# Stage one of a six-stage decoder kernel: decay weights beside the convolution, part of the sum on VectorE, out projection inside the mixing loop

## The chip, the cores and the metric

One core of one Trainium2 chip runs the whole kernel. The metric is the device time of one execution in microseconds (us). PE is TensorE, PEld its weight load, DVE VectorE, ACT ScalarE, POOL GpSimd, SP the queue that issues most transfers.

## The reference, cut to what matters

The layer is `x = layernorm(x + f(x))` six times over, with six different `f`, on x of 8 x 128 x 512 in float32. Stage one is the first: a down projection to 128 features with gelu, two applications of the same state-space layer `_hydra`, a gated mix and an up projection. The sequence axis of `_hydra` is the batch axis of x (8 steps), and the 128 positions are its batch.

```python
zxbcdt = u @ in_w.T                       # z 256, xBC 288, dt 8
dt = softplus(dt2 + dt_bias)              # forward and backward
xBC = silu(causal_conv(xBC, 7 taps))      # xs 256, B 16, C 16
y_fw, y_bw = scans(xs, dt, A, B, C)       # over 8 steps, shifted by one
y = y_fw + y_bw + xs * repeat(xs @ fcD_w.T + D, 64)
yz = y * silu(z)
y = yz * rsqrt(mean(yz**2) + 1e-5) * norm_w
return y @ out_w.T                        # next layer's u
```

With 8 steps the scans are written out: y of step t is the sum over the 8 steps s of xs[s] times one weight per (t, s, head), built from B, C and exponentials of summed dt.

## The kernel before

The six stages follow one another with a barrier of all engines between them. Only `hydra_stage` (stage one) is touched. In it the 128 partitions are the positions and a "token" t is one of the 8 steps. In each of two layers (a hardware loop on every engine), in this order on TensorE:

- z and dt of token t (L268) and the convolution of token t (L275, up to seven matmuls accumulated, weights that GpSimd multiplied together at L239), t from 0 to 7, two PSUM banks each. ScalarE takes z through silu (L336) and dt out (L337), VectorE adds the bias (L382), ScalarE takes silu of the result (L339).
- Transposes of xs (L284), copied out by ScalarE (L344), and the skip products (L289).
- Meanwhile VectorE makes the weights: softplus (L386 to L400), distances (L403 to L407), exponents (L408, L411), exp on ScalarE (L347), B times C (L414, L416), decays times dt (L419), fourteen small products along diagonals (L431, L432), skip (L435).
- The mixing loop: for token t VectorE multiplies all of xs by the weights (L442, 128 x 2048, two buffers), TensorE adds the eight products by eight matmuls with the identity (L298), VectorE multiplies by z (L448), ScalarE squares and sums (L352).
- After all eight tokens: mean square (L450), power -0.5 on GpSimd (L248), scaling (L453), transposes of y (L306), copies with norm_w (L356), out projection of both halves (L311), copies to uT (L360). Then layer 1 begins.

After layer 1 VectorE forms x times 2 plus the up bias (L456), mixes (L461, L462), TensorE projects up (L319), VectorE adds (L466). Meanwhile, in layer 0, GpSimd splits the context for stage two into a high and a low part (L243, L245), four pieces of 1024 columns each.

A matmul in full float32 is two instructions in the records, so eight matmuls are "x16". All waits are semaphores on constants or loop registers; the order on each engine is the order written.

Of the kernel before, what the change touches and what calls it, by code (L numbers as in the profile page):

```python
# [11 lines left out]
ACT = mybir.ActivationFunctionType  # L12
AX = mybir.AxisListType.X

P = 128
B, S, D = 8, 128, 512
# [121 lines left out]
def hydra_stage(nc, m, io, sem):  # L138
    with ExitStack() as ctx:
# [3 lines left out]
        def pb(name, n=HALF):  # L143
            return ctx.enter_context(nc.psum_tensor("hy_" + name, [P, n], FP32))

        xT0 = m.pre[:, :].rearrange("p (c n) -> p c n", c=KC)
# [18 lines left out]
        uT = sb("uT", [P, TOK])  # L165
        z_act = sb("z_act", [P, L, DIN])
# [11 lines left out]
        prod = [sb(f"prod{i}", [P, L, DIN]) for i in range(2)]  # L178
        yz = sb("yz", [P, L, DIN])
# [4 lines left out]
        yT = sb("yT", [P, 2, TOK])  # L184
# [4 lines left out]
        ld = {n: sem("hy_ld_" + n) for n in ("x", "gelu", "in", "conv", "small", "up", "ctx", "kv")}  # L189
        s = {n: sem("hy_" + n) for n in (  # L190
            "ident", "consts", "mid", "mid_act", "u", "wconv", "alpha", "alpha_exp", "a_exp", "na", "z_mm",
            "z_out", "c_mm", "c_out", "xbc", "xs_tr", "xs_T", "skip", "chain", "pool", "sp_in", "sp_exp",
            "seg", "dec", "w_ok", "prod", "y_mm", "yz", "ssq", "msq", "rms", "yn", "y_tr", "y_T", "o_mm",
            "mixed", "up_mm", "xres", "resid", "c_hi", "c_lo")}

        with nc.Block() as block:
            @block.sync
            def _(sp_):
                for c in range(KC):
                    sp_.dma_start(xT0[:, c, :], io["xT"].rearrange("(c p) n -> p c n", p=P)[:, c, :]).then_inc(ld["x"], 16)  # L200
                sp_.dma_start(w_down[:, :, :], io["w_downT"].rearrange("(c p) n -> p c n", p=P)).then_inc(ld["gelu"], 16)
                sp_.dma_start(b_down[:, :], io["b_down"].rearrange("(p a) -> p a", a=1)).then_inc(ld["gelu"], 16)
                sp_.dma_start(w_zdt[:, 0:DIN], io["in_wT"][:, 0:DIN]).then_inc(ld["in"], 16)
# [15 lines left out]
            def _(pool):  # L219
                pool.dma_start(taps[:, :, :], io["conv_w"].partition_broadcast(P)).then_inc(ld["conv"], 16)  # L220
# [19 lines left out]
                pool.wait_ge(s["consts"], 2)  # L240
                pool.wait_ge(ld["ctx"], 16)
                for c in range(KC):
                    pool.tensor_tensor(m.cT_hi[:, c:c + 1, :], xT0[:, c:c + 1, :], bc(m.ones[:, 0:1], 2, [P, 1, TOK]), ALU.mult).then_inc(s["c_hi"], 1)  # L243
                    pool.wait_ge(s["c_hi"], c + 1)
                    pool.tensor_tensor(m.cT_lo[:, c, :], xT0[:, c, :], raw(m.cT_hi[:, c, :]), ALU.subtract).then_inc(s["c_lo"], 1)  # L245
                with pool.Fori(0, LAYERS) as i:
                    pool.wait_ge(s["msq"], i + 1)
                    pool.tensor_tensor(rms[:, :], msq[:, :], m.minus_half[:, 0:L], ALU.pow).then_inc(s["rms"], 1)  # L248

            @block.tensor  # L250
            def _(pe):
                pe.wait_ge(ld["x"], 16 * KC)
                pe.wait_ge(ld["gelu"], 32)
                for h in range(2):
                    for c in range(KC):
                        last = pe.matmul(bank[h][:, :], w_down[:, c, :], xT0[:, c, h * HALF:(h + 1) * HALF],
                                         start=c == 0, stop=c == KC - 1)
                    last.then_inc(s["mid"], 1)
                pe.wait_ge(s["wconv"], 1)
                pe.wait_ge(s["ident"], 2)  # L260
                pe.wait_ge(ld["small"], 16 * 9)
                with pe.Fori(0, LAYERS) as i:
                    pe.wait_ge(s["u"], 2 * i + 2)
                    for t in range(L):

                        if t >= 2:
                            pe.wait_ge(s["z_out"], L * i + t - 1)
                        pe.matmul(bank[t % 2][:, 0:ZDT], uT[:, t * P:(t + 1) * P], w_zdt[:, :],  # L268
                                  start=True, stop=True).then_inc(s["z_mm"], 1)
                        if t >= 2:  # L270
                            pe.wait_ge(s["c_out"], L * i + t - 1)
                        first = max(0, TAPS - 1 - t)
                        for k in range(first, TAPS):
                            src = t - (TAPS - 1) + k
                            last = pe.matmul(bank[2 + t % 2][:, 0:CONV], uT[:, src * P:(src + 1) * P], w_conv[:, k, :],  # L275
                                             start=k == first, stop=k == TAPS - 1)
                        last.then_inc(s["c_mm"], 1)
                    for t in range(L):

                        pe.wait_ge(s["xbc"], L * i + t + 1)  # L280
                        if t >= 2:
                            pe.wait_ge(s["xs_T"], L * i + t - 1)
                        for c in range(2):
                            last = pe.transpose(bank[4 + t % 2][:, c * P:(c + 1) * P], xbc[:, t, c * P:(c + 1) * P], m.ident[:, :])  # L284
                        last.then_inc(s["xs_tr"], 1)
                    for t in range(L):
                        pe.wait_ge(s["xs_T"], L * i + t + 1)
                        for c in range(2):
                            last = pe.matmul(skip_bank[:, t * NH:(t + 1) * NH], xsT[:, c, t * P:(t + 1) * P], fcd[:, c, :],  # L289
                                             start=c == 0, stop=c == 1)  # L290
                    last.then_inc(s["skip"], 1)
                    for t in range(L):

                        pe.wait_ge(s["prod"], L * i + t + 1)
                        if t >= 2:
                            pe.wait_ge(s["yz"], L * i + t - 1)
                        for src in range(L):
                            last = pe.matmul(bank[t % 2][:, 0:DIN], m.ident[:, :], prod[t % 2][:, src, :],  # L298
                                             start=src == 0, stop=src == L - 1)
                        last.then_inc(s["y_mm"], 1)  # L300
                    for t in range(L):
                        pe.wait_ge(s["yn"], L * i + t + 1)
                        if t >= 2:
                            pe.wait_ge(s["y_T"], 2 * (L * i + t - 1))
                        for c in range(2):
                            last = pe.transpose(bank[2 + t % 2][:, c * P:(c + 1) * P], yz[:, t, c * P:(c + 1) * P], m.ident[:, :])  # L306
                        last.then_inc(s["y_tr"], 1)
                    for h in range(2):
                        pe.wait_ge(s["y_T"], 2 * (L * i + L))
                        for c in range(2):  # L310
                            last = pe.matmul(bank[4 + h][:, :], w_out[:, c, :], yT[:, c, h * HALF:(h + 1) * HALF],  # L311
                                             start=c == 0, stop=c == 1)
                        last.then_inc(s["o_mm"], 1)
                pe.wait_ge(ld["up"], 48)
                for b in range(B):
                    pe.wait_ge(s["mixed"], b // 4 + 1)
                    if b >= 2:
                        pe.wait_ge(s["resid"], b - 1)
                    pe.matmul(bank[b % 2][:, :], hm[:, b * P:(b + 1) * P], w_up[:, :], start=True, stop=True).then_inc(s["up_mm"], 1)  # L319

            @block.scalar
            def _(act):
                for h in range(2):
                    act.wait_ge(s["mid"], h + 1)
                    act.activation(x_mid[:, h * HALF:(h + 1) * HALF], bank[h][:, :], ACT.Gelu, bias=b_down[:, :]).then_inc(s["mid_act"], 1)
                for h in range(2):
                    act.wait_ge(s["mid_act"], h + 1)
                    act.activation(uT[:, h * HALF:(h + 1) * HALF], x_mid[:, h * HALF:(h + 1) * HALF], ACT.Copy).then_inc(s["u"], 1)
# [4 lines left out]
                with act.Fori(0, LAYERS) as i:  # L333
                    for t in range(L):
# [3 lines left out]
                        act.wait_ge(s["c_out"], L * i + t + 1)  # L338
                        act.activation(xbc[:, t, :], xbc[:, t, :], ACT.Silu).then_inc(s["xbc"], 1)  # L339
                    act.wait_ge(s["sp_in"], i + 1)  # L340
                    act.activation(sp[1][:, :], sp[0][:, :], ACT.Exp).then_inc(s["sp_exp"], 1)
                    for t in range(L):
                        act.wait_ge(s["xs_tr"], L * i + t + 1)
                        act.activation(xsT[:, :, t * P:(t + 1) * P], bank[4 + t % 2][:, 0:DIN].rearrange("p (c n) -> p c n", c=2),  # L344
                                       ACT.Copy).then_inc(s["xs_T"], 1)
                    act.wait_ge(s["seg"], i + 1)
                    act.activation(dec[:, :, :, :, :], dec[:, :, :, :, :], ACT.Exp).then_inc(s["dec"], 1)  # L347
                    for t in range(L):
                        act.wait_ge(s["yz"], L * i + t + 1)
                        if t:  # L350
                            act.wait_ge(s["ssq"], L * i + t)
# [1799 lines left out]
```

## Time and profile before

| | us |
|---|---|
| median of 3 runs (1761.96 to 1769.78) | 1765.85 |
| profiled execution, its own time | 1768.64 |
| its span | 1766.8 |
| stage one in it | 0 to 205.4 |
| PE busy over the span | 1557.7 (88%) |
| DVE, ACT, POOL busy | 923.5, 788.7, 734.9 |

Busy time is a sum over an engine; what ends a stage is read from the timeline of that stage. The granted clock (PEclk) is a share of full speed: 1.00 is 2.4 GHz, 0.50 is 1.2 GHz.

### The profile page before, as it was taken

The numbers are of one execution on the slowest core, as the hardware profiler recorded it, in microseconds if no ns is written. First come the engines' busy times: TensorE is split into PE (matmuls) and PEld (weight loads), VectorE is DVE, ScalarE is ACT, GpSimd is POOL, SyncE is SP. The second block draws the span as 40 slices with busy tenths as digits, with TensorE's granted clock in tenths as the row PEclk, the third lists the DMA queues.
The fourth block names the chain that finished last, engine by engine and source line by source line (L and its number), as shares of the span: only waits on it lengthen the run. The fifth ranks groups of instructions, "written<-read, shape, count | busy, mean of one in ns | idle before, by whom it ended". The sixth has DMA issues, their size and how long they took to land. (4 is left out here: it accounts for less than half of the span.)

```text
span 1766.8 us, 28778 instructions
## 1 busy us (share of the span) xinstructions
PE 1557.7 (88%) x10647; PEld 1286.8 (73%) x10647; DVE 923.5 (52%) x1621; ACT 788.7 (45%) x2417; POOL 734.9 (42%) x589
## 2 busy tenths in 40 slices
PE   5888799999997699986999648999999999999836
PEld 3767497888885478875777437888888888888724
DVE  0627611333346588773567724555555555556644
ACT  2231223444443355534899714545545445445400
POOL 4100113444422599843533544555554555542210
PEclk9888899999999799998999859999999999999978
DMA  6100100100100643104000040101100110000011
GB/s 197 36 0 0 36 19 19 38 19 21 45 6 1 213 163 125 36 1 150 1 2 25 25 132 25 37 25 37 48 28 34 37 37 25 25 1 1 1 42 48
DMA packets 63474, 77.74 MB, mean 44 GB/s; under 512 B 13884, under 2 KB 43052, under 8 KB 63340
## 3 DMA queue, kind: packets, MB, share of 16 engines
q1 hardware_dynamic: 60860, 74.36, 13.3%
q8 instruction: 84, 1.38, 0.3%
q0 software_dynamic: 464, 1.32, 0.3%
q10 hardware_dynamic: 2016, 0.27, 0.1%
q14 instruction: 50, 0.41, 0.1%
HBM read 73.85 MB, written 2.10 MB: 43 GB/s over the span
## 5 line engine op out<-in xcount | busy, mean ns | idle before, releaser
L989 POOL TENSOR_TENSOR xa_rs<-xa_ms,minus_half 128x5 f32<-128x5 f32 x64 | 74.7, 1167 | 171.4 <-DVE xa_ms L1211 171.4
L972 POOL TENSOR_TENSOR xa_prob<-xa_prob,xa_inv 128x512 f32<-128x512 f32 x64 | 66.6, 1040 | 138.3 <-DVE xa_inv L1178 138.3
L605 POOL TENSOR_TENSOR xa_prob<-xa_prob,xa_inv 128x1024 f32<-128x1024 f32 x32 | 60.6, 1895 | 142.2 <-DVE xa_inv L859 142.2
L1156 ACT ACTIVATE xa_prob<-xa_prob,xa_peak 128x128 f32<-128x128 f32 x256 | 99.8, 391 | 42.5 <-DVE xa_peak L1222 42.5
L1206 DVE TENSOR_REDUCE xa_ssq<-xa_qn 128x4 f32<-128x512 f32 x64 | 43.9, 686 | 136.4 <-ACT xa_qn L1142 136.4
L1502 DVE SCALAR_TENSOR_TENSOR ff_acc<-ff_ring,ff_sT,ff_acc 128x512 f32<-128x512 f32 x140 | 100.4, 747 | 21.9 <-ACT ff_acc L1456 12.7
L71 PE MATMUL xa_qp<-xa_q_hi,xT_hi 128*128 128x512 f32 x256 | 108.0, 422 | 1.7 <-DVE xa_q_lo L1169 1.7
L1406 PE MATMUL ff_ring<-xT_hi,ff_w 128*128 128x512 f32 x224 | 93.0, 415 | 17.9 <-DVE ff_acc L1502 11.6
L71 PE MATMUL xa_rows<-xa_o_hi,xa_out_hi 128*128 128x512 f32 x256 | 101.6, 397 | 5.2 <-DVE xtok L1185 5.2
L1884 ACT ACTIVATE sa_work<-sa_work,sa_peak 128x128 f32<-128x128 f32 x256 | 99.1, 393 | 10.3 <-DVE sa_peak L1921 10.2
L72 PE MATMUL xa_qp<-xa_q_hi,xT_lo 128*128 128x512 f32 x256 | 102.4, 400 | 0.0
L73 PE MATMUL xa_rows<-xa_o_lo,xa_out_hi 128*128 128x512 f32 x256 | 102.2, 399 | 0.0
L73 PE MATMUL xa_qp<-xa_q_lo,xT_hi 128*128 128x512 f32 x256 | 102.0, 398 | 0.0
L1142 ACT ACTIVATE xa_qn<-xa_qp 128x512 f32<-128x512 f32 x64 | 38.2, 597 | 142.8 <-PE xa_qp L73 142.8
L72 PE MATMUL xa_rows<-xa_o_hi,xa_out_lo 128*128 128x512 f32 x256 | 101.6, 397 | 0.0
L1718 POOL TENSOR_TENSOR sa_work<-sa_work,sa_inv 128x1024 f32<-128x1024 f32 x32 | 60.7, 1898 | 93.9 <-DVE sa_inv L1925 93.7
L841 DVE TENSOR_REDUCE xa_peak<-xa_score 128x4 f32<-128x1024 f32 x32 | 39.1, 1223 | 115.6 <-PE xa_score L683 115.6
L1407 PE MATMUL ff_ring<-xT_lo,ff_w 128*128 128x512 f32 x224 | 91.7, 409 | 0.0
L71 PE MATMUL xa_kvp<-xa_kv_hi,cT_hi 128*128 128x256 f32 x256 | 78.8, 308 | 8.6 <-DVE xa_kv_lo L1164 8.6
L1456 ACT ACTIVATE ff_acc<-ff_ring,ff_sT 128x512 f32<-128x512 f32 x84 | 56.9, 685 | 49.8 <-PE ff_ring L1407 49.2
L73 PE MATMUL xa_kvp<-xa_kv_lo,cT_hi 128*128 128x256 f32 x256 | 73.3, 286 | 0.0
L72 PE MATMUL xa_kvp<-xa_kv_hi,cT_lo 128*128 128x256 f32 x256 | 73.1, 285 | 0.0
(390 smaller groups left out, 4820.9 us busy)
## 6 DMA issues: line engine op xcount, KB each, us to landing
xa_raw_q<-in_wq SPq DMA_DIRECT2D x8, 1024.0 KB, 5.4
xa_raw_o<-in_wo SPq DMA_DIRECT2D x8, 1024.0 KB, 5.3
ff_dn_q<-in_down_w SPq DMA_DIRECT2D x7, 512.0 KB, 3.5
ff_dn_z<-in_down_z SPq DMA_DIRECT2D x7, 512.0 KB, 5.1
ff_dn_s<-in_down_s SPq DMA_DIRECT2D x7, 512.0 KB, 6.5
pre<-in_wq SPq DMA_DIRECT2D x16, 192.0 KB, 3.3
pre<-in_wo SPq DMA_DIRECT2D x16, 192.0 KB, 3.7
sa_work<-in_w_qkvT SPq DMA_DIRECT2D x3, 1024.0 KB, 8.3
```

The source lines that it names most:

```text
L71: pe.matmul(out, a_hi, b_hi, start=first, stop=False)
L72: pe.matmul(out, a_lo, b_hi, start=False, stop=False)
L73: return pe.matmul(out, a_hi, b_lo, start=False, stop=last)
L605: pool.tensor_tensor(prob[:, t % 3, :, :], prob[:, t % 3, :, :], bc(inv[:, t % 3, :], 2, [P, Q, KEYS]), ALU.mult).then_inc(s["norm"], 1)
L972: pool.tensor_tensor(prob[:, u % 2, :, :], prob[:, u % 2, :, :], bc(inv[:, u % 2, :], 2, [P, Q, S]), ALU.mult).then_inc(s["norm"], 1)
L989: pool.tensor_tensor(rs[:, :], ms[:, :], m.minus_half[:, 0:Q + 1], ALU.pow).then_inc(s["rs"], 1)
L1156: last = act.activation(prob[:, u % 2, h, :], prob[:, u % 2, h, :], ACT.Exp, bias=peak[:, u % 2, h:h + 1], accum_out=total[:, u % 2, h:h + 1])
L1406: pe.matmul(bank[:, :], w[:, T % 3, c, a, f], m.xT_hi[:, c, cols], start=True, stop=False)
L1407: pe.matmul(bank[:, :], w[:, T % 3, c, a, f], m.xT_lo[:, c, cols], start=False, stop=True).then_inc(s["grp"], 1)
L1502: dve.scalar_tensor_tensor(acc[:, n % SETS, slot, :], ring[(8 * n + i) % RING][:, :], column(n, i), acc[:, n % SETS, slot, :], ALU.mult, A ...
L1718: pool.tensor_tensor(prob[:, u % 3, :, :], prob[:, u % 3, :, :], bc(inv[:, u % 3, :], 2, [P, HC, S]), ALU.mult).then_inc(s["norm"], 1)
L1884: last = act.activation(prob[:, t % 3, h, :], prob[:, t % 3, h, :], ACT.Exp, bias=peak[:, t % 3, h:h + 1], accum_out=total[:, t % 3, h:h + 1])
```

## The change

- The loads: w_down and its bias first, then x in two halves of columns instead of four chunks of rows. Each half of the down projection waits for its own half.
- Layer 0 reads the gelu output directly; the copies to uT (L328) are gone. The loops over the layers are unrolled.
- z and dt of all tokens come ahead of the convolution, which now uses four banks, with the transposes of xs three tokens behind it and the skip products five behind.
- VectorE makes softplus, distances, exponents and decays between the bias adds. ScalarE changes its function table more often for that.
- norm_w is multiplied into w_out once; x times 2 plus bias and the scaling of x_mid are done before layer 0 and layer 1.
- The context's high part is copied by ScalarE in layer 0's convolution instead of by GpSimd; GpSimd keeps the low part.
- Mixing: three product buffers; VectorE adds products 2 and 3 onto 0 and 1 (`halves`), TensorE adds the remaining six. Mean square, root, transposes, out projection and the transpose back to uT are done per token inside the loop. The root scales the projected rows (128 wide) and no longer yz.

The core of the diff (the helpers are the old operations, per token):

```diff
+                for h in range(2):
+                    cols = slice(h * HALF, (h + 1) * HALF)
+                    sp_.dma_start(xT0[:, :, cols], ...[:, :, cols]).then_inc(ld[f"x{h}"], 16)
...
+                for i in range(LAYERS):          # tensor
+                    for t in range(L):
+                        z_and_dt(i, t)
+                    if i == 0:
+                        pe.wait_ge(s["wconv"], 1)
+                        pe.wait_ge(s["w_out"], 2)
                     for t in range(L):
+                        conv(i, t)
+                        if t >= 3:
+                            turn_xs(i, t - 3)
+                        if t >= 5:
+                            skip(i, t - 5)
+                    for t in range(L - 3, L):
+                        turn_xs(i, t)
+                    for t in range(L - 5, L):
+                        skip(i, t)
+                    for t in range(L + 4):
+                        if t < L:
+                            mixed_sum(i, t)
+                        if 1 <= t < L + 1:
+                            turn_y(i, t - 1)
+                        if 3 <= t < L + 3:
+                            project_out(i, t - 3)
+                        if t >= 4:
+                            turn_u(i, t - 4)
...
+                    for t in range(L):           # scalar, after z, dt and exp of softplus
+                        silu_xbc(i, t)
+                        if i == 0 and 1 <= t <= KC:
+                            act.wait_ge(ld["ctx"], 16)
+                            act.activation(m.cT_hi[:, t - 1, :], xT0[:, t - 1, :], ACT.Copy).then_inc(s["c_hi"], 1)
+                        if t == 5:
+                            act.wait_ge(s["seg"], i + 1)
+                            act.activation(dec[...], dec[...], ACT.Exp).then_inc(s["dec"], 1)
+                        if t >= 3:
+                            out_xsT(i, t - 3)
+                    for t in range(L - 3, L):
+                        out_xsT(i, t)
+                    for t in range(1, L + 4):
+                        if t < L + 1:
+                            square(i, t - 1)
+                            out_yT(i, t - 1)
+                        if 3 <= t < L + 3:
+                            out_rows(i, t - 3)
+                        if t >= 4:
+                            out_uT(i, t - 4)
...
+                    softplus_in(i)               # vector
+                    conv_bias(i, 0)
+                    conv_bias(i, 1)
+                    softplus_out(i)
+                    conv_bias(i, 2)
+                    conv_bias(i, 3)
+                    conv_bias(i, 4)
+                    distances()
+                    conv_bias(i, 5)
+                    exponents()
+                    conv_bias(i, 6)
+                    decays(i)
+                    conv_bias(i, 7)
+                    mixing_weights(i)
+                    for t in range(L + 2):
                         if t < L:
+                            products(i, t)
+                            halves(i, t)         # x[:, 0:2] += x[:, 2:4]
+                        if 1 <= t < L + 1:
+                            gated(i, t - 1)
+                        if t >= 2:
+                            mean_square(i, t - 2)
```

Waits that matter: `z_and_dt(i, t)` needs the next-to-last (t = 0) or last token of the layer before, and z_out of t - 2; `conv(i, t)` needs bias add t - 4; `mixed_sum` needs `halves(t)` and `gated(t - 2)`; `products` needs the sum of t - 3; `project_out` the copied transpose; `turn_u(t)` the rows that `out_rows(t)` scales by the root; `gated(t)` the sum of t.

## Rows read from the trace of the kernel before

**Rows 1.** Stretches of stage one: us, busy by engine, granted clock (PEclk), DMA share, GB/s.
```profile
29.05:50.90 21.85, 21.09 (x88) 16.49 (x89) 3.90 (x12) 8.53 (x27) 15.31 (x8) 1.00 0.24 92
50.90:65.00 14.10, 10.21 (x48) 8.82 (x46) 12.30 (x50) 5.41 (x12) 1.55 (x1) 0.61 0.34 112
65.00:97.10 32.10, 29.69 (x128) 25.52 (x128) 20.68 (x16) 3.56 (x14) 0.00 (x0) 0.91 0.00 1
97.10:113.50 16.40, 10.97 (x24) 4.59 (x24) 2.77 (x10) 6.54 (x21) 1.68 (x1) 0.69 0.00 0
...
148.20:181.30 33.10, 30.71 (x128) 26.24 (x128) 20.66 (x16) 3.56 (x14) 0.00 (x0) 0.88 0.00 0
181.30:205.40 24.10, 17.78 (x41) 7.07 (x40) 14.92 (x23) 6.27 (x20) 1.65 (x1) 0.79 0.00 0
```
**Rows 2.** Timeline of the front, layer 0: start us, us, engine, line, operation.
```profile
17.08 10.16 PE L256 MATMUL hy_bank<-pre,hy_w_down 128*128 128x512 f32 x16 [17.08 <-DMA hy_b_down<-in_b_down]
...
27.86 1.14 ACT L328 ACTIVATE hy_uT<-hy_x_mid 128x512 f32<-128x512 f32 x2
29.02 1.28 ACT L330 ACT_TABLE_LOAD   x1
...
31.92 0.38 ACT L336 ACTIVATE hy_z_act<-hy_bank 128x256 f32<-128x256 f32 x1
...
32.59 0.39 ACT L336 ACTIVATE hy_z_act<-hy_bank 128x256 f32<-128x256 f32 x1
```
**Rows 3.** DMA issues of 0 to 60 us: KB each, median us from issue to landing.
```profile
pre<-in_xT SPq DMA_DIRECT2D x4, 512.0 KB, 6.6
...
hy_b_up<-in_b_up SPq DMA_DIRECT2D x1, 256.0 KB, 8.5
```
**Rows 4.** Timeline, end of the first convolution up to the mixing.
```profile
47.33 3.56 PE L275 MATMUL hy_bank<-hy_w_conv,hy_uT 128*128 128x288 f32 x14
...
50.10 2.36 POOL L245 TENSOR_TENSOR cT_lo<-pre,cT_hi 128x1024 fp32r<-128x1024 f32 x1
...
50.92 0.46 DVE L382 TENSOR_TENSOR hy_xbc<-hy_bank,hy_conv_b 128x288 f32<-128x288 f32 x1 [3.38 <-PE hy_bank L275]
51.30 1.24 DVE L386 TENSOR_TENSOR hy_sp<-hy_dt_raw,hy_dt_bias 128x64 f32<-128x64 f32 x1
```
**Rows 5.** Timeline from 60 us, the mixing weights and the mixing of layer 0.
```profile
60.23 1.22 DVE L414 TENSOR_TENSOR hy_cb_prod<-hy_xbc 128x1024 f32<-128x1024 f32 x1
...
65.00 4.49 DVE L442 TENSOR_TENSOR hy_prod<-hy_xbc,hy_mixw 128x2048 f32<-128x2048 f32 x2
...
67.35 29.69 PE L298 MATMUL hy_bank<-hy_prod,ident 128*128 128x256 f32 x128 [3.45 <-DVE hy_prod L442]
72.91 0.42 DVE L448 TENSOR_TENSOR hy_yz<-hy_bank,hy_z_act 128x256 f32<-128x256 f32 x1 [3.41 <-PE hy_bank L298]
...
76.36 0.42 DVE L448 TENSOR_TENSOR hy_yz<-hy_bank,hy_z_act 128x256 f32<-128x256 f32 x1 [0.83 <-PE hy_bank L298]
```
**Rows 6.** Groups by line and form, 0 to 206 us: busy us, mean ns of one.
```profile
L442 DVE TENSOR_TENSOR hy_prod<-hy_xbc,hy_mixw 128x2048 f32<-128x2048 f32 x16 | 36.4, 2283 | 0.1
...
L408 DVE TENSOR_TENSOR hy_dec<-hy_seg,hy_neg_a 128x448 f32<-128x448 f32 x2 | 1.2, 624 | 0.1
```
**Rows 7.** Timeline, end of stage one.
```profile
134.72 0.21 DVE L386 TENSOR_TENSOR hy_sp<-hy_dt_raw,hy_dt_bias 128x64 f32<-128x64 f32 x1
...
196.41 1.96 PE L319 MATMUL hy_bank<-hy_w_up,hy_hm 128*128 128x512 f32 x4 [0.37 <-DVE hy_hm L462]
...
204.66 0.69 DVE L466 TENSOR_TENSOR xtok<-xtok,hy_bank 128x512 f32<-128x512 f32 x1 [0.17 <-PE hy_bank L319]
```
**Rows 8.** Timeline of a later stage: eight transposes between matmuls at full clock.
```profile
419.72 1.09 PE L694 MATMUL xa_turn<-ident,xa_prob 128*128 128x128 f32 x8
420.57 0.48 PE L71 MATMUL xa_rows<-xa_wide_hi,cT_hi 128*128 128x512 f32 x1
```
**Rows 9.** Source line 1583: count, duration ns min/median/max.
```profile
L1583 POOL TENSOR_TENSOR rstd<-var,minus_half x32: 547/555/782, 516.7 to 1690.4; 128x1 f32<-128x1 f32 x32
```

More of the change, by code:

```diff
@@ new lines, in conv @@
+                def conv(i, t):
+                    u = uT if i else x_mid
+                    if t >= 4:
+                        pe.wait_ge(s["c_out"], L * i + t - 3)
+                    first = max(0, TAPS - 1 - t)
+                    for k in range(first, TAPS):
+                        last = pe.matmul(bank[2 + t % 4][:, 0:CONV], u[:, token(t - (TAPS - 1) + k)], w_conv[:, k, :],
+                                         start=k == first, stop=k == TAPS - 1)
+                    last.then_inc(s["c_mm"], 1)
@@ new lines, in turn_xs, with skip @@
+                def turn_xs(i, t):
+                    n = L * i + t
+                    pe.wait_ge(s["xbc"], n + 1)
+                    pe.wait_ge(s["z_out"], L * i + L)
+                    if t >= 2:
+                        pe.wait_ge(s["xs_T"], n - 1)
+                    for c in range(2):
+                        last = pe.transpose(bank[t % 2][:, c * P:(c + 1) * P], xbc[:, t, c * P:(c + 1) * P], m.ident[:, :])
+                    last.then_inc(s["xs_tr"], 1)
+                def skip(i, t):
+                    pe.wait_ge(s["xs_T"], L * i + t + 1)
+                    for c in range(2):
+                        last = pe.matmul(skip_bank[:, t * NH:(t + 1) * NH], xsT[:, c, token(t)], fcd[:, c, :], start=c == 0, stop=c == 1)
+                    last.then_inc(s["skip"], 1)
@@ L260, in _ @@
                 pe.wait_ge(s["ident"], 2)
-                pe.wait_ge(ld["small"], 16 * 9)
-                with pe.Fori(0, LAYERS) as i:
-                    pe.wait_ge(s["u"], 2 * i + 2)
+                for i in range(LAYERS):
                     for t in range(L):
[L266 to L277, printed above, removed]
-                    for t in range(L):
[L280 to L313, printed above, removed]
@@ L323, in _, with out_uT @@
+                def out_uT(i, t):
+                    act.wait_ge(s["u_tr"], L * i + t + 1)
+                    act.activation(uT[:, token(t)], bank[t % 2][:, DM:2 * DM], ACT.Copy).then_inc(s["u"], 1)
                 for h in range(2):
                     act.wait_ge(s["mid"], h + 1)
[L325 to L328, printed above, removed]
+                    act.activation(x_mid[:, h * HALF:(h + 1) * HALF], bank[2 + h][:, :], ACT.Gelu, bias=b_down[:, :]).then_inc(s["mid_act"], 1)
@@ L332, in _ @@
                 act.activation(neg_a[:, :], a_log[:, :], ACT.Exp).then_inc(s["a_exp"], 1)
-                with act.Fori(0, LAYERS) as i:
+                for i in range(LAYERS):
                     for t in range(L):
```

242 lines of the change are left out of this document (153 added, 89 removed).

## The prediction

> **What bounds the kernel now.** I read the stretches of stage one first, since the change touches nothing else; the barrier behind it makes every microsecond saved there one off the span. The stretches are cut where the work changes: convolution, weights, mixing, tail, and again for layer 1 [rows 1]. In the convolution TensorE is busy for 21.1 of 21.9 us at full clock; it is the bound. In the weights' stretch (50.9 to 65.0) VectorE is busy for 12.3 of 14.1 us and TensorE waits for it in the end. In the mixing TensorE is busy for 29.7 of 32.1. In the tail (97.1 to 113.5) nobody is busy for long: a chain of VectorE, ScalarE, GpSimd, power, scaling, transposes, projection, with the clock at 0.69 of full. Layer 1 repeats it, with a tail of 24.1 us that includes the up projection. So stage one is 205.4 us in which two kinds of stretch are latency: weights (14.1 us, twice) and tails (16.4 and 24.1 us).
>
> **The front.** The down projection starts at 17.08, when a tiny bias load that is queued behind x lands, and takes 10.16 us, two thirds of it in the first half [rows 2]. Afterwards the weights and the bias come first. The pieces of x (512 KB) landed 6.6 us after issue in the median [rows 3]; half an x (two such pieces) behind w_down I put at 8.6 us, the second half at 14.5. Bounds: 6 us, and 17.1 us, the present start. First half 8.6 to 15.4, second to 18.8. ScalarE then does gelu, a table load (1.28 us), two tiny exponentials, another load, and the first silu of z. Before, the first silu was at 31.92, 4.7 us after the down projection's end at 27.24; without the two copies (together 1.14) that is 3.6, so with 18.8 for the end it is 22.4, say 22.5. The silus are 0.66 us apart [rows 2]. z of token 7 has two banks and waits for token 5, so at 26.5, and the convolution begins at 27.0. VectorE does x times 2 plus bias early; it waits for a load that landed at 24.3 (issued at 15.8, 8.5 us [rows 3]) and takes some 4.4 us (as long as two products, [rows 5]), till 28.7: it holds up the first bias add, but four banks cover that.
>
> **Convolution with decays.** 14 instructions take 3.4 us (47.33 to 50.7) [rows 4], so the 70 of a layer 17.0. Between them lie five pairs of transposes and three of skip products, four instructions each; 128-column instructions at full clock are 0.106 us apart (eight from 419.72 to 420.57) [rows 8], 0.43 a group, 3.4 in all: 20.4 us a layer. TensorE is half idle in the z phase, so I add 1.8 us of half clock in layer 0 and 1.4 in layer 1 (bounds 0 and 2.8: the first sum of layer 0, cold, took 72.91 - 67.35 = 5.6 us, the next 3.45 [rows 5]). VectorE's work beside it, what was done in the weights' stretch without its last 3.9 us, plus eight bias adds of 0.46, is about 12 us: hidden under 20. Behind the convolution stay: last bias 0.5, last silu 0.5, products of B and C, reduction, diagonals, skip: 65.00 - 60.23 less the two decay products of 0.4, 3.9 us; together 5.0 for 14.1 and 13.9.
>
> The added waits of VectorE: softplus waits for ScalarE's exp behind a table load, and bias adds 2 to 7 are queued behind it. TensorE's convolution of t waits only for bias add t - 4, so 6 us of slack. The table loads for the exp of the decays and back to silu (1.28 each) lie between bias 5 and bias 7, with two convolutions (7 us) as cover. If that cover were gone they would cost 2.6 us.
>
> **The port.** In layer 0 GpSimd's low parts (2.36 us each, four) now fall beside VectorE's small two-input operations. The same addition took 1.24 us at 51.30, where GpSimd's piece ran from 50.10 to 52.46, and 0.21 us in layer 1 where GpSimd was idle [rows 4, 7]. So they block. Most of the 9.4 us falls into VectorE's 8 us of slack; I take 1.0 (bounds 0 and 4). The page "SBUF — State Buffer" of the Trainium skill, section "Who interferes with whom", says the shared port pair is an exclusive lock held for the whole instruction; the pair of durations agrees. Taken alone it would add the 9.4 us and sixteen roots of 0.55 us, 18.2 us less whatever is slack.
>
> **Mixing.** Before, a token took 3.45 us (72.91 to 76.36), eight sums of two instructions, 0.216 each, VectorE idle for 0.83 of it [rows 5]. Now TensorE: 12 x 0.216 = 2.59, five transposes and projections of 128 columns 1.07, 3.66 a token. VectorE: product 2.28 with its result waited for, the half-sum of 512 elements (448 took 0.62) 0.65, gating 0.35, mean square 0.15: 3.45 [rows 6]. The two are level; the loop does not get shorter. First product and half-sum 2.95, cold first sum 5, then VectorE's pace for two tokens and TensorE's for the rest: last sum at 31.8 after the start, against 32.1 and 33.1. The root per token takes 0.55 us on GpSimd [rows 9] and may hold the port against the half-sum: 0.15 a token, 1.2 us a layer (bounds 0 and 0.35 a token). So 33.0 a layer.
>
> **The tails.** After the last sum: gating 0.5, transposes 0.5, square and copy 0.5 more on ScalarE, then projection, scaled rows, transpose and copy for tokens 5, 6 and 7 alternate between TensorE and ScalarE at about 0.7 a token: 4.2 us until layer 1's z (bounds 3.5 and 7), for 16.4. After layer 1 the up projection can start at 3.9 instead of 15.1 us, and what follows it takes 8.9 us as before (196.41 to 205.35) [rows 7]: 12.7 for 24.1. The 1.0 us of x_mid scaling on VectorE lies under the first.
>
> **Sum** (before, after): convolution starts 29.1, 27.0 (z now ahead of it); it ends 50.9, 27.0 + 20.4 + 1.8 = 49.2; mixing starts 65.0, 49.2 + 5.0 + 1.0 = 55.2; last sum 97.1, 88.2; layer 1 starts 113.5, 92.4; its convolution starts 5.0 later (ScalarE's silus), 97.4, and ends 134.3, 119.2; mixing 148.2, 124.2; last sum 181.3, 157.2; end 205.4, 169.9. That is 35.5 us less: 1768.64 - 35.5 = 1733.1 for an execution like the profiled one, and 1730 for the median, which stands 2.8 us below it.
>
> **Rivals.**
> 1. The port is worse: GpSimd's pieces reach the bias adds and the last silu (3 us more) and the root stretches VectorE's pace to 4.0 us, beyond TensorE's 3.66 (3 us more), with some delay of the roots themselves (1.5): 7.5 off the gain, 28, so 1738. For it: the 1.24 us [rows 4]. Against: 8 us of slack, and a root that reads one column. By the page's lock (SBUF — State Buffer), every root would also wait for a running product.
> 2. The halves of x land no earlier than 17 us, because GpSimd's small loads share the engines: the down projection ends at 27 as before, 8 us lost, 1739. For it: 8.5 us for a quarter of a megabyte. Against: the first pieces of x, which landed at 6.6 us after issue.
> 3. Slower: TensorE's clock stays at its low level in the mixing loop, where it now waits for four partners per token. At 1.2 GHz a token is 7.3 us; 16 x (7.3 - 3.45) = 62 us lost, 35.5 gained: 1792. It decides from a pace of 5.7 us a token (35.5 / 16 above 3.45) on. Against: the clock rose in the first sum of both layers and stayed at full (0.91 and 0.88 with the cold start in it) [rows 1], and TensorE is as busy as before.
> 4. The change doesn't overlap as written: a wait in the wrong order (say bias add 5 behind the distances, these behind GpSimd) makes TensorE stand in the convolution, and both tails take 7 us and more. With 1 and 2 that leaves a gain under 9 us, 1757 and more, which is what a measurement here can barely tell from none (0.5%).
>
> **How the numbers follow.** Forecast with its own spread (1720 to 1737) 0.64; rival 1 0.14; rival 2 0.12; both or long tails (1743 to 1757) 0.04; rival 3 0.02; rival 4 0.04. Bounds: all terms at their good ends give 44 us of gain, 1722; clock, tail and port at their bad ends together take some 12 off, 1742. The range of 1719 to 1745 takes in rivals 1 and 2. Faster by over 0.5% 0.94, within 0.5% 0.04, slower 0.02.
>
> **What would show it.** Right: down projection starting near 9 us; last bias add to first product 4.5 us; sums 3.5 to 3.8 us apart; layer 1's z about 4 us after the last gating; stage two at 170. Wrong: VectorE operations of 64 elements above 1 us throughout layer 0 (rival 1); TensorE idle between convolutions for bias adds; a granted clock of 0.5 inside the mixing (rival 3); half-sums above 1 us; GpSimd roots above 2 us.

## The result, and the profile after

The changed kernel takes 1743.84 us in the median of 4 runs (1741.07 to 1748.08); the kernel before, 1767.57 in 4 (1761.96 to 1769.78). The ratio is 0.9873, with a 95% interval of 0.984 to 0.9905: faster by 23.7 us, where 35.9 was forecast against the median shown then (1765.85 to 1730), and the time lies inside the range, near its upper end. A second series of the changed kernel (e0 below) gave 1742.28 against 1770.24, ratio 0.9844 (0.9827 to 0.986), a gain of 28.0 us.

| profiled execution, us | before | after | forecast |
|---|---|---|---|
| its own time | 1768.64 | 1741.07 | 1733.1 |
| span | 1766.8 | 1739.2 | |
| stage one ends | 205.4 | 176.3 | 169.9 |
| the rest of the span | 1561.4 | 1562.9 | unchanged |

The distance to the forecast median adds up: 1730 was 3.1 below the profiled sum; stage one kept 6.4; the rest of the span came out 1.5 longer (in the eleven profiles of changed kernels it is 1561 to 1568, so 1.5 is within their scatter); and this profiled run stands 2.8 below its own median. 3.1 + 6.4 + 1.5 + 2.8 = 13.8. The 3.1 came from a median of three runs, 2.8 below the profiled execution. With its fourth run that median is 1767.57, 1.1 below it, and in the later series of seven and nine runs it is 1770.24 and 1769.98, above it: so little or nothing should have been taken off.

Stage one in stretches cut at the same events as in [rows 1] (first convolution matmul, last bias add, first product, last gating, layer 1's z), and the columns are those of [rows 1]:

```profile
31.79:52.90 21.11, 19.57 (x92) 15.11 (x91) 18.28 (x40) 12.85 (x23) 9.39 (x4) 1.00 0.11 35
52.90:58.60 5.70, 3.97 (x29) 3.45 (x28) 4.28 (x18) 3.13 (x8) 0.00 (x0) 0.90 0.42 150
58.60:90.24 31.64, 28.00 (x129) 23.88 (x130) 26.01 (x30) 7.06 (x27) 13.21 (x6) 0.86 0.00 1
90.24:96.97 6.73, 4.22 (x26) 3.19 (x24) 1.51 (x5) 3.08 (x12) 1.42 (x2) 0.85 0.00 0
96.97:103.47 6.50, 6.37 (x17) 3.76 (x17) 0.00 (x0) 3.29 (x15) 0.00 (x0) 0.63 0.00 0
103.47:122.50 19.03, 19.03 (x91) 15.10 (x89) 9.91 (x40) 10.57 (x21) 0.00 (x0) 1.00 0.00 1
122.50:127.68 5.18, 4.30 (x31) 3.93 (x30) 4.37 (x19) 1.65 (x5) 0.00 (x0) 0.81 0.00 0
127.68:159.23 31.55, 27.60 (x129) 23.54 (x130) 26.01 (x29) 6.94 (x27) 13.18 (x6) 0.87 0.00 1
159.23:176.30 17.07, 13.83 (x41) 6.38 (x39) 7.58 (x13) 3.35 (x13) 1.56 (x2) 0.80 0.00 1
```

The two latency stretches shrank as argued: behind the convolution 5.7 and 5.2 us for 14.1 and 13.9; the tails 6.7 and 17.1 for 16.4 and 24.1. Three things stand out against the forecast: the convolution starts at 31.8, not 27.0; VectorE's 40 instructions take 18.3 us beside layer 0's convolution and 9.9 beside layer 1's, with GpSimd's four pieces (9.39 us) only in the first; and the granted clock is 0.63 in layer 1's z phase.

The front, from the timeline of after:

```profile
13.83 10.11 PE L333 MATMUL hy_bank<-pre,hy_w_down 128*128 128x512 f32 x16 [13.83 <-DMA pre<-in_xT]
...
27.59 0.38 ACT L415 ACTIVATE hy_z_act<-hy_bank 128x256 f32<-128x256 f32 x1
```

and from its DMA issues, columns as in [rows 3]:

```profile
pre<-in_xT SPq DMA_DIRECT2D x2, 1024.0 KB, 11.9
...
hy_w_down<-in_w_downT SPq DMA_DIRECT2D x1, 256.0 KB, 2.5
hy_b_down<-in_b_down SPq DMA_DIRECT2D x1, 0.5 KB, 2.7
```

w_down and its bias were there in 2.7 us, but the halves of x, 1024 KB each, took 11.9 us from issue in the median; the second half's matmuls follow without a wait. VectorE in layer 0's convolution, with GpSimd beside it, timeline of after:

```profile
41.88 0.17 DVE L475 TENSOR_TENSOR hy_seg<-hy_seg,hy_dt 128x16 f32<-128x16 f32 x1
42.03 7.03 POOL L254 TENSOR_TENSOR cT_lo<-pre,cT_hi 128x1024 fp32r<-128x1024 f32 x3 [2.56 <-ACT cT_hi L423]
42.08 2.35 DVE L473 TENSOR_TENSOR hy_seg<-hy_seg,hy_dt 128x12 f32<-128x12 f32 x1
...
44.54 2.21 DVE L473 TENSOR_TENSOR hy_seg<-hy_seg,hy_dt 128x8 f32<-128x8 f32 x1
...
46.87 2.21 DVE L473 TENSOR_TENSOR hy_seg<-hy_seg,hy_dt 128x4 f32<-128x4 f32 x1
```

A step of 16 columns takes 0.17 us, and a smaller one 2.35 when a piece of GpSimd's has begun before it: one such step per piece, three in a row here. The fourth, a step of 64 columns at 37.16, took 2.39 us beside the first piece. The bias adds are queued behind these steps. TensorE feels that by a detour: ScalarE's silus wait for the bias adds, its copies of the transposed xs (L378) are queued behind the silus (and behind copies of the context, 1.04 us each, which e2 below keeps without such a wait), and the next transposes, which need the bank that is copied out, stand in TensorE's queue ahead of the next convolution:

```profile
40.57 0.44 ACT L374 ACTIVATE hy_xbc<-hy_xbc 128x288 f32<-128x288 f32 x1 [3.53 <-DVE hy_xbc L447]
...
43.65 0.41 PE L288 MATMUL hy_bank<-ident,hy_xbc 128*128 128x128 f32 x2 [1.07 <-ACT hy_xsT L378]
...
52.43 0.41 PE L288 MATMUL hy_bank<-ident,hy_xbc 128*128 128x128 f32 x2 [0.47 <-ACT hy_xsT L378]
```

These two waits, and a last bias add that starts at 52.90, 0.9 us after the last convolution matmul, are why this stretch takes 21.1 us where layer 1's takes 19.0.

The end of the tail, timeline of after:

```profile
90.25 0.61 PE L321 MATMUL hy_bank<-hy_w_out,hy_yT 128*128 128x128 f32 x4
...
91.91 0.68 PE L321 MATMUL hy_bank<-hy_w_out,hy_yT 128*128 128x128 f32 x4 [0.72 <-ACT hy_uT L403]
92.43 0.27 PE L327 MATMUL hy_bank<-ident,hy_u_tok 128*128 128x128 f32 x1
93.64 0.68 PE L321 MATMUL hy_bank<-hy_w_out,hy_yT 128*128 128x128 f32 x4 [0.94 <-ACT hy_uT L403]
94.17 0.27 PE L327 MATMUL hy_bank<-ident,hy_u_tok 128*128 128x128 f32 x1
95.05 1.20 PE L321 MATMUL hy_bank<-hy_w_out,hy_yT 128*128 128x128 f32 x4 [0.61 <-ACT hy_uT L403]
```

The projection is released not by its input, but by the copy of the turned rows to uT (L403) of two tokens before: both live in `bank[t % 2]`, in its two halves, and `project_out` waits for `u` of t - 2 (L321). That makes it about 1.7 us a token, and TensorE idles more than half of it. At 95.05 the projection of the same size takes 1.20 instead of 0.68: the granted clock has fallen to 0.50 (0.50 in 96.00 to 98.00). From 92.00 to 94.00 TensorE had been busy for 1.06 us of 2.

### The profile page after: what moved, and what is told of

The parts are those of the page before. It is cut to its first block and busy times, and to the rows that moved or that the text cites. A ratio compares the mean times of both kernels' runs of the same rounds, so it can differ in the third digit from the quotient of the medians.

```text
span 1739.2 us, 28763 instructions
## 1 busy us (share of the span) xinstructions
PE 1533.5 (88%) x10647; PEld 1269.9 (73%) x10647; DVE 937.7 (54%) x1637; ACT 800.0 (46%) x2437; POOL 753.0 (43%) x599
## 3 DMA queue, kind: packets, MB, share of 16 engines
q1 hardware_dynamic: 61340, 74.36, 13.5%
## 5 line engine op out<-in xcount | busy, mean ns | idle before, releaser
L1627 DVE SCALAR_TENSOR_TENSOR ff_acc<-ff_ring,ff_sT,ff_acc 128x512 f32<-128x512 f32 x140 | 100.4, 747 | 22.2 <-ACT ff_acc L1581 13.5
```

Source lines behind the costliest of these rows:

```text
L1627: dve.scalar_tensor_tensor(acc[:, n % SETS, slot, :], ring[(8 * n + i) % RING][:, :], column(n, i), acc[:, n % SETS, slot, :], ALU.mult, A ...
```

## The experiments

The theories before them. **A** (the ports): GpSimd's low parts block VectorE's small steps and cost more than the 1.0 us taken. **B** (a shared bank): the tails are long through the wait for uT, and the low clock of what follows is its consequence. Rivals: **C**, the loads (x comes late, and this is the shortfall); **D**, VectorE's half-sums or the roots stretch the loop; **E**, the parts I credited with the gain are not what gives it. No kernel leaves anything of the output out. e1 to e7 are single runs, and the eight runs of the changed kernel spread over 1740.87 to 1748.08, so for e1, e2, e3, e5 and e7 the totals decide little and I go by the stretches of stage one. The experiments lie on three chips, on which the kernel before took 1770.24 (e0, e1, e2, e7), 1770.69 (e3 to e6) and 1769.98 us (e9, e10).

**e0, the changed kernel again**, as the control.

> The changed kernel once more, as the base of the comparisons. Theory A (stage one alone is different, and its schedule repeats): stage one ends within 0.5 us of 176.3, and the rest of the span differs from run to run by some microseconds, as it does before the change (1762 to 1770). Theory B (the later stages have become slower through the change): the stretch behind stage one is again 1.5 us longer than before or more.

1742.28 us (1740.87 to 1747.34), ratio to before 0.9844 (0.9827 to 0.986). Its profile gives the spread of one order of work, wider than the 0.5 us that I expected: stage one 179.6 (176.3 in the first), because the first convolution starts at 33.3 and the twenty skip products behind it run at a low clock (4.27 us for them, 2.67 in the first profile), so that the first product waits:

```profile
61.69 0.19 DVE L507 TENSOR_TENSOR hy_mixw<-hy_skip_bank,hy_d_skip 128x32 f32<-128x32 f32 x1 [1.72 <-PE hy_skip_bank L294]
```

Differences of 3 us between single profiles therefore need an event to hang on; I compare distances between events. The rest of the span is 1565.9 here, 4.5 more than in the profile of the kernel before, which is what theory B of this expectation asked for. Against it: the median span of the kernel before in this series is 1768.4, which less 205.4 leaves 1563.0 by estimate, and the eleven changed kernels have 1564.1 in the mean. Of the kernel before there is one profile only, so it is likely, and not shown, that the later stages lost no more than about a microsecond.

**e1, GpSimd's small loads behind x** (rival C):

```diff
+                pool.wait_ge(ld["x0"], 16)
                 pool.dma_start(taps[:, :, :], io["conv_w"].partition_broadcast(P))...
```

> GpSimd issues its loads (taps and the small ones) only when the first half of x has landed. Theory A (the small loads hold up x, as rival 2 of the prediction has it): the first matmul starts at 7 to 10 us instead of 13.8; stage one ends up to 4 us earlier if the taps and small loads still come in time, else the down projection is early and the gate's exponentials wait. Rival (x in two halves of columns is slow by itself, 2 KB pieces): the first matmul stays at 12 to 14 us, and stage one gets 5 to 10 us longer because everything on GpSimd is late.

1745.65 us, stage one 178.0, between after and e0: no gain that can be told. But x does come as forecast:

```profile
8.98 9.75 PE L334 MATMUL hy_bank<-pre,hy_w_down 128*128 128x512 f32 x16 [8.98 <-DMA pre<-in_xT]
...
24.91 0.20 ACT L410 ACTIVATE hy_sp<-hy_gate 128x1 f32<-128x1 f32 x1 [4.16 <-DMA hy_w_out<-in_out_wT]
```

and from its DMA issues

```profile
pre<-in_xT SPq DMA_DIRECT2D x2, 1024.0 KB, 7.1
```

So GpSimd's loads (nine small ones and the 1008 KB of broadcast taps) do hold up x, 11.9 us in after and up to 14.7 in e6 against 7.1 here. Made late, they hold up ScalarE, whose two exponentials stand ahead of the first silu: 26.63, only 1 us ahead of after's 27.59. The wait changes its name.

**e7, the loads in the old order** (x in four chunks ahead of w_down, one wait for all of it; the change of the loads undone).

> Undoes one part: x is loaded in four chunks of rows ahead of w_down, and both halves of the down projection wait for all of it. Theory A (the new order of loads is worth what the start moved, 3.3 us): first matmul at 17.1 instead of 13.8, stage one 3 us longer. Rival (the first silu of z or the x-times-2 pass on VectorE, held by its own load, sets the layer's start anyway): stage one within 1 us of the changed kernel.

1740.2 us, stage one 177.2. The down projection starts at 16.92, when the bias queued behind x lands, the convolution at 35.8, 2.5 us after e0's and 4.0 after after's. At the first product 1.9 against e0 are left; then layer 0's loop (30.7 for 31.6), its tail (6.1 for 6.7) and layer 1's z phase (5.0 for 6.35, granted clock 1.00 for 0.66) gave 2.8 back. But the start scatters: in the nine other profiles with the new order of loads and GpSimd's loads beside them the down projection starts at 13.8 to 16.6, the convolution at 31.4 to 35.1 (e6). So the new order is worth 0.7 to 4.3 us at the convolution by this one run, against the 8.5 that I had put on the start of the down projection (17.08 to 8.6), and in the total it can't be told from nothing.

**e2, GpSimd's low parts behind layer 0's roots** (theory A), when VectorE is past its small steps:

```diff
-                for c in range(KC):
-                    pool.wait_ge(s["c_hi"], c + 1)
-                    pool.tensor_tensor(m.cT_lo[:, c, :], ...)
                 for i in range(LAYERS):
                     for t in range(L):
                         root(L * i + t, t)
+                    for c in range(KC if i == 0 else 0):
+                        pool.wait_ge(s["c_hi"], c + 1)
+                        pool.tensor_tensor(m.cT_lo[:, c, :], ...)
```

> GpSimd makes the context's four low parts behind the roots of layer 0, where VectorE is idle, and not beside the convolution. Theory A (the port is what delays the mixing of layer 0): none of VectorE's small operations takes over 1 us, the first product starts 2 to 3 us earlier (56 instead of 58.6), stage one ends 2 to 3 us earlier. Rival (TensorE's convolution and the last bias add set the start of the mixing, the port is hidden): the first product stays within 0.5 us of 58.6.

1739.83 us. From the first convolution matmul to the first product 24.2 us, against 26.8 (after), 28.6 (e0), 28.7 (e1), 28.4 (e3) and 28.0 (e7). The steps that took 2.2 are 0.17 again, and the bias adds wait for TensorE, not the other way round:

```profile
42.85 0.17 DVE L473 TENSOR_TENSOR hy_seg<-hy_seg,hy_dt 128x12 f32<-128x12 f32 x1
...
48.77 0.46 DVE L447 TENSOR_TENSOR hy_xbc<-hy_bank,hy_conv_b 128x288 f32<-128x288 f32 x1 [2.58 <-PE hy_bank L277]
```

The ports cost 2.6 us against after and 4.4 against e0, of which 2.1 lie in the convolution; the rest lies behind it, where the late copies leave transposes and skip products, in e0 at a low clock. A holds, and after is the mildest case: the seven other profiles with GpSimd's pieces beside VectorE's steps have 28.0 to 28.7, e9 23.9. The total is within the scatter of the changed kernel; e9 below confirms the stretch a second time.

**e3, a bank of its own for the turned rows** (theory B); `project_out` then waits only for the scaled rows of t - 2, `turn_u` for the copy of t - 1:

```diff
-                        pe.wait_ge(s["u"], n - 1)
+                        pe.wait_ge(s["o_out"], n - 1)
...
+                    if n >= 1:
+                        pe.wait_ge(s["u"], n)
-                    pe.transpose(bank[t % 2][:, DM:2 * DM], ...)
+                    pe.transpose(u_bank[:, (t % 2) * DM:(t % 2 + 1) * DM], ...)
```

> The transposed rows get a PSUM bank of their own, so that the projection of token t no longer waits for the copy of token t - 2. Theory A (that wait makes the tails 6.7 us and not the predicted 4.2): layer 1's first z comes 1.5 to 3 us earlier after the last gating, and the up projection too; stage one ends 3 to 5 us earlier. Rival (the latencies of ScalarE's four copies per token make the tail, with whatever bank): under 1 us.

1737.01 us, stage one 171.0, 8.6 less than e0's. The last gating to layer 1's z takes 4.43 us (6.73), to the end of the stage 13.1 (17.0), and the clock stays up in both stretches:

```profile
92.90:97.33 4.43, 3.40 (x25) 2.80 (x24) 1.52 (x5) 2.98 (x12) 1.42 (x2) 1.00 0.00 0
97.33:102.36 5.03, 5.03 (x17) 2.47 (x17) 0.00 (x0) 3.42 (x15) 0.00 (x0) 1.00 0.00 0
```

With 13.1 to the end of the stage these are close to the forecast's 4.2, 12.7 and 5.0. B holds.

**e10, TensorE kept busy in the tail**, the bank as in the changed kernel. e3 takes away the wait and the low clock together; this is to take away the clock alone, with multiplications of the identity by itself into a spare bank:

```diff
                         if 3 <= t < L + 3:
                             project_out(i, t - 3)
+                            if t >= L:
+                                for _ in range(2):
+                                    pe.matmul(spare[:, :], m.ident[:, :], m.ident[:, :], start=True, stop=True)
```

(and the same behind `turn_u`).

> The changed kernel with four idle-filling multiplications a token (identity by identity into a spare bank) on TensorE in the tail of each mixing loop, behind the projections of the last five tokens; nothing else moves, and TensorE waited 0.6 to 0.9 us a token there. If the low clock behind the tail comes from TensorE standing idle in it, the granted clock stays at 1.00 there, layer 1's z phase takes 5.0 us instead of 6.5 and the up projection 7.8 instead of 9.6, while the shared bank's waits stay (y7 to z1 6.0 to 6.9 us): some 3 us off the stage, a median of 1738 to 1741. If the clock falls for another reason, both stretches stay at 6.5 and 9.6, and the added multiplications at half clock make the tail up to 2 us longer.

1743.91 us (1737.47 to 1748.8), ratio to before 0.9852 (0.9819 to 0.9885): not the 1738 to 1741 that I expected, and in the total no difference that the interval could show. In the stretches there is one (last gating to z, the z phase, the up projection):

```profile
93.06:100.24 7.18, 6.40 (x54) 5.87 (x53) 1.52 (x5) 3.55 (x13) 1.43 (x2) 1.00 0.00 0
100.24:105.08 4.84, 4.28 (x19) 2.56 (x17) 0.00 (x0) 2.96 (x14) 0.00 (x0) 1.00 0.01 3
167.53:176.05 8.52, 7.75 (x18) 2.37 (x16) 6.25 (x9) 0.03 (x1) 0.00 (x0) 1.00 0.00 0
```

The tail keeps the bank's wait and gets 0.45 us longer (7.18 for 6.73; I had expected 6.9 at most), the clock is 1.00, the z phase 4.8 (6.5), the up projection and what follows it 8.5 (10.3). So the low clock is worth 1.7 + 1.8 us of the stage, less what the added multiplications cost in the tails. That it comes from TensorE's idling in the tail fits, but rests on this one profile: of the eight profiles with the shared bank and nothing added, the z phase was spared in one (e7, 5.0) and the stretch from the up projection on in two (e5 and e6, 8.6), for which no run shows a reason. e3 and e9, whose tails wait less, had 1.00 in all four stretches. Of e3's 8.6 us against e0, 2.3 and 2.5 are waits in the two tails, 1.3 and 1.6 the clock behind them, and some 1 lies elsewhere.

**e9, e2 and e3 together.**

> Two causes taken out at once: GpSimd writes the low halves of cT behind the roots of layer 0 instead of beside VectorE's small steps, and the out projection has a bank of its own, apart from the one that the rows are turned in. If the shortfall of the forecast lay in these two places, and they are independent, the gains of each alone add up: from the last control's 1742.3 us some 3.5 us for the ports (in layer 0, from the first convolution matmul to the first product, 24.2 where the control took 28.6) and 7 us for the tails (the last gating to layer 1's z 4.4, to the end of the stage 13.1, and a z phase of 5.0 at full clock), so 1731 to 1735 us, stage one ending near 168 us, a ratio to the kernel before of 0.980. If instead the part that the port cost turns up again in the first layer's loop or at the stage's end, the median stays at e3's 1737 and the stage at 171.

1731.52 us (1729.1 to 1736.13), ratio to before 0.9783 (0.976 to 0.9806), stage one 165.8. The intervals of e0 and e9 don't touch: the two repairs are worth 10.8 us in the median, and they add up: the stretch from convolution to first product shrinks from e3's 28.4 to 23.9, and e3's stage less these 4.5 is 166.5. This is the fastest version of the study.

**e4, the decays behind the convolution** (rival E: is it the overlap that pays?). Softplus, distances, exponents and decays follow the eight bias adds.

> Undoes one part: VectorE makes softplus, distances, exponents and decays behind the eight bias adds, as before the change; ScalarE's two exponentials move with them (two table loads less per layer). Theory A (the decays were on the path and now lie under the convolution): from the last bias add to the first product 13 to 14 us instead of 5.7 and 5.2, in layer 0 partly less because the port is free there; stage one 14 to 17 us longer. Rival (the convolution is slowed by the interleaving, by late bias adds): the convolution gets 2 us or more shorter and stage one is under 12 us longer.

1761.73 us against 1770.69 for the kernel before beside it: two thirds of the gain are gone. From the start of layer 1's convolution to its first product it takes 33.8 us (24.5 in e0), stage one 195.7 (+16.1 to e0, of which 1.3 is a later start of the first convolution). In layer 0 the same stretch grew by 5.5 only, as the ports' cost went with it (VectorE's two-input steps of 4 to 64 columns take 0.15 to 0.25 us here): against e2 it is 9.9.

**e5, all eight products added on TensorE** (theory D), `halves` gone.

> Undoes one part: TensorE adds all eight products, VectorE none. Theory A (VectorE at 3.32 and TensorE at 3.37 a token are level, so the half-sums let TensorE carry the projection): a token takes 16 x 0.216 + 0.77 = 4.2 us, the loops get 5 to 6 us longer each, the start 0.7 us shorter, stage one 9 to 12 us longer. Rival (something else paces the loop, such as the 2.5 us roots): a token stays at 3.3 to 3.6 us and stage one within 3 us.

1746.89 us, within the spread of the changed kernel. The loops take 36.4 and 36.1 us instead of 31.6, 4.8 more each: TensorE is the bound now, with 3.67 us for a token without a projection and 4.23 with one (84.42 to 88.65). Of the 9.6 us against e0 much is hidden: the first convolution started 1.9 earlier, the stretch behind the second loop is 2.5 us shorter, 1.6 of them in the up projection, whose clock stayed at 1.00 here, and three shorter stretches behind the first loop make 1.6. The stage is longer by 3.8 (183.4 against e0's 179.6), not by the 9 to 12 expected. In the loops the half-sums pay for themselves: they don't stretch them, they shorten them.

**e6, the rows' work behind the loop**: all sums first, then transposes, projections and copies for eight tokens (yz for eight; hm placed in z_act).

> Undoes one part: the transposes of y, the out projection, scaling and transposing back come behind the eight sums instead of between them (root and mean square stay per token; yz has eight buffers, hm lies in z_act). Theory A (the per-token chain in the tail is paced by its shared bank at 1.7 us a token, and the loop hides five of eight): the loop runs at VectorE's 3.32 us, the tail becomes 8 x 1.7, about 13 us, instead of 6.7, stage one 10 to 14 us longer. Rival (the tail is cheap wherever it stands, 0.7 a token): the tail grows by under 4 us and the loop gets shorter, so that stage one is within 5 us.

1762.95 us. Last gating to layer 1's z 14.25 us (+7.5 to e0), from it to the end in layer 1 22.2 (+5.0), stage one 193.1 (+13.5, of which 1.8 is a later start of the first convolution). Each projection again waits for L403:

```profile
100.85 0.68 PE L321 MATMUL hy_bank<-hy_w_out,hy_yT 128*128 128x128 f32 x4 [0.72 <-ACT hy_uT L403]
102.58 0.68 PE L321 MATMUL hy_bank<-hy_w_out,hy_yT 128*128 128x128 f32 x4 [0.72 <-ACT hy_uT L403]
```

That is 1.73 us a token, five tokens more than in the changed kernel: 8.7 expected from it, 7.5 seen.

## Why the prediction was right or wrong

The direction, the place and the two sources of the gain were right, and e4 and e6 show it: the decays beside the convolution give 14.8 us in the two stretches of e4, the out projection inside the loop 12.5 in the two of e6, and without either more than half of the gain is gone. The steps that failed are terms of the sum: the first half of x at 8.6 us (13.8 measured), the port at 1.0 (2.6 to 4.4), the tails at 4.2 and 12.7 (6.7 and 17.1), and no low clock behind the tails (1.7 and 1.8).

Stage one gained 29.1 us in the profiles where 35.5 was forecast. Too short in the sum were the front by 4.8, the tails by 2.5 and 4.4, layer 1's z phase by 1.5, layer 1's stretch behind the convolution by 0.2, together 13.4; too long were the convolutions by 1.1 and 2.8, layer 0's stretch behind it by 0.3 and the loops by 1.4 each, together 7.0. That half of the first group was cancelled by the second is luck, and the time of 1743.84 lies where the prediction had put "both or long tails (1743 to 1757)", with a chance of 0.04. Of the five signs of being right none came within its number: 13.8 for 9, 5.7 and 5.2 for 4.5, 3.3 for 3.5 to 3.8, 6.7 for 4, 176.3 for 170. In order:

- **The front** failed: 8.6 us for the first half of x. I scaled from chunks that stood at the head of the queue; here each half of 1 MB came in 11.9 us beside GpSimd's loads (e1: 7.1 without them). The convolution starts 4.8 late. Rival 2 happened in part (x at 13.8, not after 17; 4.8 us lost of its 8), and e1 shows that loading x early alone would not have paid, since a second wait stands behind it.
- **Convolution**: 70 instructions and the transposes take 19.0 us in both layers where nobody disturbs (layer 1, e2), not 22.2 and 21.8. The half clock that I added didn't come (granted 1.00), and a transpose of 128 columns is one instruction in the trace (L288 x2 for a pair), not two, as I had counted. In layer 0 the port's 2.1 us lie in this stretch, and the price of 22.2 covered them by chance.
- **The port** was mis-sized: 1.0 us was taken, 2.6 to 4.4 measured (e2), up to the upper bound of 4 and a little beyond. "Most falls into slack" was the wrong step: slack was counted in busy time, but the bias adds are queued behind the blocked steps in order, and ScalarE's silus and copies behind them. The page "SBUF — State Buffer" of the Trainium skill, section "Who interferes with whom", says that whoever issues first keeps the pair for the whole instruction; each blocked step ends with GpSimd's piece, as that says (the step of 42.08 at 44.43; the first of the three pieces, a third of 7.03 us from 42.03 on, at 44.4). The sum of 18.2 by the page alone would have been far too much: the roots cost nothing (below).
- **Behind the convolution**: 5.7 and 5.2 for 6.0 and 5.0. Right in this profile; in layer 0 the seven other profiles with GpSimd's pieces beside VectorE's steps have 6.9 to 7.6, by the late copies and the low clock that the ports leave behind.
- **The loop**: 31.6 for 33.0, both layers. The two engines are level: VectorE works without a gap, 3.32 us from product to product (74.18, 77.50), and TensorE takes 3.36 for a token (84.08 to 87.44), 12 x 0.216 and seven instructions of 0.11, where I had 3.66. The half-sum took 0.69, near the forecast of 0.65. The working itself had a slip: its parts, 2.95, 5, two tokens at 3.45 and five at 3.66, make 33.15 and not 31.8, before the 1.2 for the roots.

```profile
76.49 0.69 DVE L523 TENSOR_TENSOR hy_prod<-hy_prod 128x512 f32<-128x512 f32 x1
...
77.50 2.28 DVE L514 TENSOR_TENSOR hy_prod<-hy_xbc,hy_mixw 128x2048 f32<-128x2048 f32 x1
77.54 0.39 ACT L391 ACTIVATE hy_yT<-hy_bank 128x256 f32<-128x256 f32 x1 [2.80 <-PE hy_bank L321]
77.66 2.53 POOL L230 TENSOR_TENSOR hy_rms<-hy_msq,minus_half 128x1 f32<-128x1 f32 x1 [0.79 <-DVE hy_msq L535]
```

- **The root** did not hold up VectorE (price 0, not 0.15 a token): it comes behind the product, so GpSimd waits, 2.53 us for a root of 0.55, and the rows that need the root are scaled a token later, which covers that. "GpSimd roots above 2 us", which I had named as a sign of being wrong, was seen and cost nothing; VectorE's steps above 1 us, the sign of rival 1, were seen four times and not throughout, and did cost time.
- **The tails** failed: 4.2 us forecast (its named parts, three of 0.5 and three of 0.7, make 3.6), 6.73 measured, and 12.7 against 17.0, inside the bound of 7 that I had put on the first. "About 0.7 a token" left out that projection and turned rows share a bank. The wait was in the diff (`project_out` waits for `u` n - 1); I listed "the copied transpose" for it and not this. With its own bank 4.4 and 13.1 (e3).
- **The clock** was not in the tail's sum at all: z phase 6.5 for 5.0, and 1.8 us in the up projection (e10).
- **Clock low in mixing** (rival 3) did not happen: a sum came each 3.3 us, and the loop's mean clock was 0.86 with its cold start in it. Of rival 4 (no overlap as written) TensorE's waits in the convolution were seen, 1.5 us of them, and a tail of 6.7 where it said 7 and more, but not its loss of the gain.

Seen so, that e9 ends at 1731.5, near the forecast of 1730, is partly an accident: the front's 5 us are still missing there (convolution from 31.7, not 27.0), and convolutions 3.2 and 2.4 us and loops 1.4 us each under their prices make up for them.

## What to carry to other kernels

When work is moved beside other work, write for every moved wait which bank, buffer and queue it shares, not only which result it needs: here a half bank saved cost 2.3 and 2.5 us in the two tails, and the clock that fell behind them some 1.3 and 1.6 more. Slack on an in-order queue is the time until the next instruction that somebody waits for, not the engine's idle share; a chain of short VectorE steps with two inputs is best kept clear of GpSimd pieces that are long against them. And a tail on which TensorE idles may be paid twice, in waiting and in the clock of what comes next.

## What the runs showed of the hardware

- A VectorE step of 12 columns took 2.35 us beside a GpSimd subtraction of 1024 columns, 0.17 without it; the other way round, a GpSimd root of one column took 2.53 us beside a VectorE product of 2048 (0.55 alone), and the product kept its 2.28. In both pairs the instruction that came first kept its time and the other ended with it or after it.
- The granted clock fell to 0.50 behind a tail in which TensorE was busy for 1.06 us of 2, and layer 1's z phase took 6.35 to 6.5 us in the changed kernel, e0, e1, e2, e4 and e6 and 5.9 in e5; in e7, with the same order of work in the tail, it took 5.0 at 1.00. With four small multiplications a token (e10, one profile) it stayed at 1.00.
- x landed 11.9 us after its issue on the sync queue beside GpSimd's loads (11.9 to 14.7 in the nine profiles with this order of loads), and 7.1 without them.
- Four table loads of ScalarE a layer (1.28 us each) cost nothing that can be seen in layer 1: TensorE is busy for all of the 19.03 us of its convolution, beside which they run.
